# SiLU of a convolution as one ScalarE function for two chunks at a time, with VectorE's products at other steps

## What is computed

```python
xr = x @ in_proj_w.T
xf, res = jnp.split(xr, [D_INNER], axis=-1)          # 512 inner channels each
xf = jax.nn.silu(_causal_dw_conv(xf, conv_w, conv_b))
y = _ssm(xf, res, x_proj_w, dt_proj_w, dt_proj_b, A_log, D)
xb = jax.nn.silu(_causal_dw_conv(xf, conv_b_w, conv_b_b))
y_b = _ssm(xb, res, ..., reverse=True)
return (y + y_b) @ out_proj_w.T
# in _ssm:  delta = softplus(...);  xs = cumsum(dB_u * dA_cum) / (dA_cum + 1e-12)
#           y = einsum('bldn,bln->bld', xs, C) + u * D;  return y * silu(res)
```

## Time and profile before

| | |
|---|---|
| median of 3 runs | 5794.56 us (5793.66 to 5795.1) |
| the profiled execution | 5799.28 us |
| its span | 5797.5 us |
| scan of step 0, first and sixth sequence | 93.97 us, 1560.14 us |
| from one sequence to the next, the last ten | 293.5 to 293.6 us |
| second stage | from 4788.7 us on |
| busy: TensorE, VectorE, GpSimd, ScalarE | 87%, 79%, 75%, 71% |

### The profile page before, as it was taken

How to read it: one execution, slowest core, us unless ns; L and a number is a source line. 1 busy time by engine, 2 the same in 40 slices (tenths; PEclk the granted TensorE clock), 3 DMA queues, 4 the chain that set the end, 5 groups by cost and what they waited for, 6 DMA issues and landing times. The chain is left out here.

```text
span 5797.5 us, 50924 instructions
## 1 busy us (share of the span) xinstructions
PE 5046.3 (87%) x14776; PEld 2599.2 (45%) x14776; DVE 4606.2 (79%) x4075; ACT 4095.2 (71%) x6465; POOL 4365.2 (75%) x2136
## 2 busy tenths in 40 slices
PE   6888888888888888888888889898989897999999
PEld 2444443434343434344444444343434344656578
DVE  5898989898989898989898989898989891222235
ACT  4888888888888888888888888888888883111100
POOL 4898989899999999999999999999999990000000
PEclk8999999999999999999898989898989898999999
DMA  2444444444444444444443434344444442344356
GB/s 85 126 135 127 136 129 133 130 134 133 134 129 133 129 133 130 133 129 134 127 137 126 134 128 137 126 136 130 132 131 128 138 126 75 106 133 126 95 174 214
DMA packets 555605, 755.30 MB, mean 130 GB/s; under 512 B 124091, under 2 KB 272443, under 8 KB 553277
## 3 DMA queue, kind: packets, MB, share of 16 engines
q1 hardware_dynamic: 540765, 737.36, 40.7%
q10 hardware_dynamic: 14560, 14.68, 0.8%
HBM read 662.04 MB, written 89.82 MB: 130 GB/s over the span
## 5 line engine op out<-in xcount | busy, mean ns | idle before, releaser
L643 POOL TENSOR_TENSOR g_ring<-dtu,b_ring 128x1024 f32<-128x1024 f32 x1026 | 2422.5, 2371 | 342.9 <-DVE e_ps L995 315.7
L995 DVE TENSOR_TENSOR_SCAN e_ps<-e_ps,g_ring 128x1024 f32<-128x1024 f32 x1024 | 2343.6, 2289 | 44.5 <-ACT e_ps L798 30.5
L652 POOL TENSOR_TENSOR v_ring<-z_ring,c_ring 128x1024 f32<-128x1024 f32 x768 | 1818.8, 2370 | 19.7 <-issue 19.7
L1154 PE MATMUL y_ps<-v_ring,ident 128*128 128x512 f32 x3088 | 1602.3, 628 | 262.1 <-DVE res_gate L978 253.1
L798 ACT ACTIVATE e_ps<-dt,a_neg 128x512 f32<-128x512 f32 x2050 | 1327.2, 680 | 364.6 <-DVE v_own L1017 254.4
L808 ACT ACTIVATE f_ring<-rsum,consts,a_neg_half 128x512 f32<-128x512 f32 x2052 | 1551.6, 806 | 36.6 <-DVE e_ps L1008 33.6
L1154 PEld LDWEIGHTS y_ps<-v_ring,ident 128*128 128x128 f32 x3088 | 583.7, 202 | 888.1 <-issue 656.8
L1008 DVE SCALAR_TENSOR_TENSOR z_ring<-f_ring,e_ps 128x1024 f32<-128x1024 f32 x768 | 936.4, 1219 | 52.9 <-issue 0.9
L1154 PE MATMUL y_ps<-v_own,ident 128*128 128x512 f32 x1028 | 540.7, 622 | 0.0
L1084 PE MATMUL side<-u,conv_diag 128*128 128x512 f32 x1088 | 494.9, 598 | 20.7 <-ACT disp_ring L759 11.3
L1324 ACT ACTIVATE x_act<-x_ps,x_bg 128x512 f32<-128x512 f32 x128 | 88.1, 688 | 570.7 <-PE x_ps L1383 570.7
(11 more groups left out here) (135 smaller groups left out, 5134.2 us busy)
## 6 DMA issues: line engine op xcount, KB each, us to landing
b_ring<-bc_scr SPq DMA_DIRECT2D x1027, 256.0 KB, 3.7
c_ring<-bc_scr SPq DMA_DIRECT2D x1025, 256.0 KB, 3.4
pT_scr<-rowT_ring SPq DMA_DIRECT2D x136, 256.0 KB, 4.1
m_pT<-pT_scr SPq DMA_DIRECT2D x16, 2048.0 KB, 8.4
sT_scr<-sT_ring SPq DMA_DIRECT2D x272, 64.0 KB, 2.7
x_xT<-sT_scr SPq DMA_DIRECT2D x16, 1024.0 KB, 9.2
eo_scr<-x_eo SPq DMA_DIRECT2D x32, 512.0 KB, 5.1
m_eo<-eo_scr ACTq DMA_DIRECT2D x14, 1024.0 KB, 6.9
```

The source lines that it names most:

```text
L643: pool.tensor_tensor(g_ring[:, k], dtu[d][:], both(b_ring[:, k:k + 1]), ALU.mult).then_inc(g_done, 1)
L652: pool.tensor_tensor(v_slot(i), z_ring[:, k], both(c_ring[:, k:k + 1]), ALU.mult).then_inc(v_pool, 1)
L995: dve.tensor_tensor_scan(e, e, g, 0.0, ALU.mult, ALU.add).then_inc(scan_done, 1)
L1154: pe.matmul(y_ps[:, t % 2], ident[:], v, start=(t % (TILES // PAIRS) < 2), stop=True, skip_group_check=True).then_inc(v_used, 1)
```

## The change

SiLU of both convolutions is taken with ScalarE's own function, straight from the bank to `u`, with the whole bias. This is done for two chunks in a row, when the second (i odd) is due three tiles after its fill; each frees its bank. Identity, Tanh, VectorE's product and the halved bias go. The products on VectorE are made at steps 0, 4, ..., 60 (the new expression gives these) instead of 1, 5, ..., 61, and EARLY is (20, 52) instead of (21, 53). In the list AHEAD conv1_0 comes behind dt0, which alters the order before the first sequence alone. That v's slots are now counted over all sequences changes nothing, as 16 and 48 products a sequence fill their rings of 4 and 6 evenly.

```diff
 AHEAD = tuple((kind, i) for kind in ("in0", "conv0") for i in range(4)) + (
-    ("x0", 0), ("conv1", 0), ("dt0", 0), ("dt0", 1)) + tuple(("conv1", i) for i in range(1, 4)) + (("x1", 0),)
+    ("x0", 0), ("dt0", 0), ("dt0", 1)) + tuple(("conv1", i) for i in range(4)) + (("x1", 0),)
...
-    EARLY = (21, 53)
-    ON_DVE = [i for i in range(STEPS) if i % 4 == 1]
+    EARLY = (20, 52)
+    OWN = 16
+    ON_DVE = [i for i in range(STEPS) if (i * OWN + OWN // 2) // STEPS != ((i - 1) * OWN + OWN // 2) // STEPS]
...
-                    elif kind in ("conv0", "conv1"):
-                        bias = b_conv_half[:, d, i:i + 1]
-                        act.activation(u[d][:, i, PAD:], src, ACT.Identity, scale=0.5, bias=bias).then_inc(half_done, 1)
-                        act.wait_ge(half_done, at.nth(s, ("conv0", "conv1")))
-                        act.activation(src, src, ACT.Tanh, scale=0.5, bias=bias).then_inc(tanh_done, 1)
+                    elif kind in ("conv0", "conv1") and i % 2 == 1:
+
+                        act.activation(u[d][:, i - 1, PAD:], side[:, at.bank(s - 1)], ACT.Silu,
+                                       bias=b_conv[:, d, i - 1:i]).then_inc(side_free[at.bank(s - 1)], 1)
+                        act.activation(u[d][:, i, PAD:], src, ACT.Silu, bias=b_conv[:, d, i:i + 1]).then_inc(free, 1)
...
-                if kind in ("conv0", "conv1") and lag == 4:
-                    d = int(kind[-1])
-                    dve.wait_ge(tanh_done, at.nth(s, ("conv0", "conv1", "res")))
-                    dve.scalar_tensor_tensor(out=u[d][:, i, PAD:], in0=src, scalar=1.0,
-                                             in1=u[d][:, i, PAD:], op0=ALU.add, op1=ALU.mult).then_inc(free, 1)
```

More of the change, by code:

```diff
@@ L290, in sequence_stage @@
         w_in = sb("w_in", [P, KM, 2 * DI])
-        b_conv_half = sb("b_conv_half", [P, NDIR, KI])
+        b_conv = sb("b_conv", [P, NDIR, KI])
         w_x = sb("w_x", [P, NDIR, KI, XR])
@@ L357, in sequence_stage @@
         tanh_done = sem("tanh_done")
-        half_done = sem("half_done")
         dt_done, dtu_done, cut_done = sem("dt_done"), sem("dtu_done"), sem("cut_done")
@@ L443, in _ @@
                 sp.dma_start(dst, src).then_inc(w_loaded, 16)
-            for dst, src in ((b_conv_half, conv_b), (w_x, x_wT), (a_neg, A_log)):
+            for dst, src in ((b_conv, conv_b), (w_x, x_wT), (a_neg, A_log)):
                 sp.dma_start(dst[:], src).then_inc(w_loaded, 16)
@@ L650, in times_c @@
                 pool.wait_ge(z_done, b * STEPS + (i + 1 + CR))
-                pool.wait_ge(v_used, b * TILES + (2 * (same_slot_before(i) + 1) + CR))
-                pool.tensor_tensor(v_slot(i), z_ring[:, k], both(c_ring[:, k:k + 1]), ALU.mult).then_inc(v_pool, 1)
+                pool.wait_ge(v_used, 2 * (same_slot_before(b * STEPS + i) + 1) + CR)
+                pool.tensor_tensor(v_slot(b * STEPS + i), z_ring[:, k], both(c_ring[:, k:k + 1]), ALU.mult).then_inc(v_pool, 1)
             def variances(now):
@@ L890, in _ @@
             dve.wait_ge(ident_done, 2)
-            dve.tensor_scalar(b_conv_half[:], b_conv_half[:], 0.5, None, ALU.mult)
             for d in range(NDIR):
@@ L911, in side_step @@
                 if kind == "res" and lag == 3:
-                    dve.wait_ge(tanh_done, at.nth(s, ("conv0", "conv1", "res")))
+                    dve.wait_ge(tanh_done, at.nth(s, ("res",)))
                     dve.scalar_tensor_tensor(out=res_gate[:, i], in0=res_gate[:, i], scalar=1.0, in1=src,
                                              op0=ALU.add, op1=ALU.mult).then_inc(free, 1)
-                if kind in ("conv0", "conv1") and lag == 4:
-                    d = int(kind[-1])
-                    dve.wait_ge(tanh_done, at.nth(s, ("conv0", "conv1", "res")))
-                    dve.scalar_tensor_tensor(out=u[d][:, i, PAD:], in0=src, scalar=1.0,
-                                             in1=u[d][:, i, PAD:], op0=ALU.add, op1=ALU.mult).then_inc(free, 1)
                 if kind in ("dt0", "dt1"):
@@ L1015, in times_c @@
                     dve.wait_ge(c_loaded[k], b * (RING.count(k) * 16) + (RING[:i].count(k) + 1) * 16)
-                    dve.wait_ge(v_used, b * TILES + (2 * (same_slot_before(i) + 1) + CR))
-                    dve.tensor_tensor(v_slot(i), e_ps[:, i % 2], both(c_ring[:, k:k + 1]), ALU.mult).then_inc(v_dve, 1)
+                    dve.wait_ge(v_used, 2 * (same_slot_before(b * STEPS + i) + 1) + CR)
+                    dve.tensor_tensor(v_slot(b * STEPS + i), e_ps[:, i % 2], both(c_ring[:, k:k + 1]), ALU.mult).then_inc(v_dve, 1)
                 for t in range(TILES):
@@ L1152, in add_state @@
                         pe.wait_ge(y_gated, b * PAIRS + (t // (TILES // PAIRS) + 1))
-                v = v_slot(i)[:, t % 2]
+                v = v_slot(b * STEPS + i)[:, t % 2]
                 pe.matmul(y_ps[:, t % 2], ident[:], v, start=(t % (TILES // PAIRS) < 2),
```

## The result

| | median | ratio to before, 95% interval |
|---|---|---|
| before | 5794.83 us (beside the runs of after) | |
| after | 5752.04 us (5749.96 to 5753.91, 4 runs) | 0.9925 [0.9907, 0.9942] |

The change made the kernel 43 us faster. The forecast was 5836 us, 41 us slower, so it missed by 84 us, or 5.2 us a sequence. The profiled execution took 5751.63 us (span 5749.9). From one sequence to the next it is now 290.13 us in most, where it was 293.55.

A forecast was written before the change was run, and what follows sets the result against it. Four engines nearly full, so the order of work decides. Per sequence -1.4 + 2.0 - 1.2 - 0.6 + 3.7 = +2.5 us, 40 for sixteen, 41 with the start: forecast 5836 us, range 5730 to 5882.

The forecast's parts named there:

- rival B: SiLU lies in the table set of Exp and Tanh, so no loads, a pair 1.28 us: 5695 us, chance 0.08.
- A pair then holds ScalarE 1.28 + 2.57 = 3.85 us in one piece: Each SiLU pair: two SiLUs plus two table loads hold ScalarE 3.85 us after the fill, formerly 2.7 us in two.
- a drain of about 1.38 us: Rival: two switches drained at each of two exposed pairs, 5.5 us more a sequence, near 5924 us; chance 0.01.
- The first and second pair: SiLU pairs of steps 22 to 30: ScalarE's holds make the scan of step 30 later, +2.0 us a sequence.
- The third and fourth pair: SiLU pairs counted from the scan of step 44: the scan of step 51 comes later, +3.7 us a sequence.
- Step 16: GpSimd's product before its deviation chain goes, so the scan's wait for ScalarE shortens: -1.4 us a sequence.
- Steps 16 to 22: Stretch before the first pair: no term of its own in the sum, 0 us a sequence.
- Step 36: VectorE's product moves ahead of the gate's 4.06 us wait, none after it at step 37: -1.2 us a sequence.
- The product u of conv0_2: At step 43 VectorE leads and this product was on its path; removing it gives -0.6 us a sequence.
- Steps 20 to 22: Step 20's product falls free before a 2.10 us wait; conv0_0's fill loses its 0.70 us wait.
- C: Rival: TensorE's clock falls if new waits grow beyond about 2 us, +3 us a sequence: 5885 us, chance 0.13.
- A: Rival: ScalarE's slack at steps 25 and 50 absorbs the pairs, the moves remain, -3.2 us a sequence: 5744 us, chance 0.21.

The follow-up runs named there:

- loads exposed: After, with an always-met wait holding the load behind the fill and a one-element Exp calling the load back at once: 5837.6 us, ratio 1.0071.
- moves alone: Kernel before with only the ON_DVE steps (0, 4, ...) and EARLY (20, 52) changed, SiLU in its old form: 5725.9 us, ratio 0.9877.
- after with two reductions: After with two unread reductions of 128x512 (1.35 us) added on VectorE at step 58 of each sequence: 5773.4 us, ratio 0.9961.
- SiLU alone: After with VectorE's products back at steps 1, 5, ... and EARLY at (21, 53), SiLU pairs kept: 5809.3 us, ratio 1.0021.

## Why the forecast was wrong

*What bounded the kernel* was read rightly: the order of the work between four nearly full engines. The events at which a cost was put are the ones at which the runs show it.

*The function tables.* The assumption that SiLU needs two loads of 1.283 us a pair held (rival B fell), and so did 0.69 and 0.60 for the SiLUs (1.27 us for two against 1.28). The first step that failed is the next sentence of the forecast, "A pair then holds ScalarE 1.28 + 2.57 = 3.85 us in one piece". Behind the fill it held ScalarE 1.27 us at the second pair, and 2.57 at the first. That both loads stand behind the fill was taken for granted. The loads of Softplus in the earlier trace rows couldn't show it, with 3.1 us of idle time before 65 of them and 0.7 before the Softpluses: ScalarE hardly waits there. The number of loads had bounds from both sides in the forecast, their place had none, and 0 us past the fill would have been its other end. The load runs ahead of the wait, and the load back is put off to the next Exp, since SiLU's table serves Tanh as well. The Trainium skill, page "ScalarE: Activation LUTs", section "What ACT_TABLE_LOAD costs", adds a drain of about 1.38 us to each switch. Behind the load it doesn't show here either, since a decay starts 1.30 us behind the start of the load ahead of it (1679.50 to 1680.80), which is the load's own 1.28. Whether SiLUs taken one by one would cost more loads than pairs, no run here shows.

*The first and second pair*, +2.0 us from step 16 to step 30. The marks moved by +1.4 us there with the loads exposed and by -3.4 in after. Only the part from step 22 on is the pairs': +0.3 in after, so the forecast had it 1.7 us too dear. *The third and fourth pair*, +3.7 us from step 44 to 51: +4.4 with the loads exposed, +1.8 after, so 1.9 too dear.

*Steps 16 to 22*, put at nothing, are the second step that failed. In after they are 3.0 us shorter in the mean. Two things are in that. At the same granted clock of 0.89 they take 32.15 us in before (its fifth sequence) and 31.15 in after, and 31.0 in the moves alone, so 1 us is the moves'. The rest is the clock: 0.89 in most sequences of after, with in0's fill in 3.7 us, and 0.82 in most of before, at 34.9 us.

*The moves.* Step 16: -1.4 forecast, -1.36 measured. Step 36: -1.2 against -0.9 (step 34 to 38 at a granted clock of 0.93, 23.37 us in after and in the moves alone, 24.25 in before). The product u of conv0_2: -0.6 against -0.60 (after, step 38 to 44, beside the moves alone, where it is 0.0). Steps 20 to 22 were in the forecast as a free product and 0.7 us for conv0_0's fill, and both were taken up into the +2.0 at step 30. The moves alone stand at -3.18 there, 1.8 us beyond step 16's share (1.0 of it from step 22 to 30, at full clock): that part of their worth is in no term of the sum.

*TensorE's clock* was a rival only as a loss (C, a longer wait that costs a fill). It moved the other way: in after the in0 fill is at full clock in 12 sequences of 16, in before in one, its fifth, and that one took 291.06 us and not 293.55. This was in the trace of before, and I didn't look for what made one sequence shorter. Inside one kernel the period differs with it by 2.5 us a sequence (before), 3.4 (after), 1.5 (after with two reductions). It isn't the only such place: SiLU alone has the fill at full clock in 14 sequences of 16 and a period of 293.55 us, with 25.6 us from step 34 to 38 at 0.87.

*The rivals.* A had the median nearly right (5744 us) and its sign, for part of the right reason: what lies past the fill nearly fits the slack at steps 22 to 30 (+0.3 us), though not before step 51 (+1.8). But it isn't because a hold of 3.85 us is absorbed; the run with both loads exposed shows that such a hold is not. And the median came near it partly by luck, as steps 16 to 22 made up for what the pairs still cost.

The 84 us divide by the table of stretches, after less the forecast's terms. Of 5.5 us a sequence 3.6 are the pairs' hold (1.7 from step 22 to 30, 1.9 from 44 to 51), 3.0 are steps 16 to 22, and 1.0 goes the other way, 0.85 of it behind step 51. That the run with both loads exposed accounts for all of it (86 us) is again partly the clock, since its steps 16 to 22 lost 2.1 us against after. What exactly makes a given order of work settle in one pattern, I can't tell from these runs.

## What to carry to other kernels

In these traces a table load waits for nothing but its place in ScalarE's program: what falls in idle time ahead of the function is hidden, and a set that also serves the functions behind it puts the return off. Here 2.8 of 10.3 us of loads were paid. So price a load by where it stands against the waits, not by the count. Compare runs stretch by stretch, and first in stretches whose length is the same in every sequence. Try the parts of a change by themselves: here two lines of step numbers are worth 72 us and the new function next to it costs 26. And where a pipeline's stages are this tight, a difference of up to 1% between two versions (290.13 against 293.55 us, in one execution) may be TensorE's clock falling in another place, so compare the period, and one fixed fill, sequence by sequence, before a cost is put down to an instruction.

## What the runs showed of the hardware that I had not expected

- An ACT_TABLE_LOAD isn't held by the wait of the function it is for: 17.9 us of idle time before 66 loads, all of it before the sixteen sequences, and 62.9 us before the 68 SiLUs. With a second wait in the program it is held: 144.3 us before the loads.
- SiLU's table also serves Tanh, Copy and Identity: three of four pairs go on with a guard and a copy (L739, L744) or an Identity (L749) before any load, and no load stands there at L808 that isn't Softplus's (48, as before).
- The same eight matmuls behind the same 2.07 us of idle time took 3.70 or 5.40 us in following sequences of one execution, and the sequences 290.13 or 293.55 us.
- Steps 34 to 38 took 21.7, 23.4 and 24.2 us at a granted clock of 1.00, 0.93 and 0.86, in the moves alone and in the run with both loads exposed alike; VectorE, ScalarE and GpSimd were busy the same in each to 0.1 us.
- 21.6 us of added VectorE work on its leading stretch cost 3 us (-2 to +9) in the kernel before.
